# Converting and turning the next graph's adjacency earlier in a four-layer graph kernel

## The chip, the cores and the metric

The kernel runs on one core of a Trainium2 chip. The metric is the device time of one execution in microseconds. The engines are named as the profile names them: PE (TensorE matrix multiplies) with PEld (its weight loads), DVE (VectorE), ACT (ScalarE), POOL (GpSimd), and SP (SyncE), which issues the DMA transfers. The engines run their own instruction lists in order and meet only at semaphores.

## The reference, cut to what matters

There are 16 graphs of 512 nodes with 64 features each. Four graph layers follow one another, each with a residual and a layer norm. The change touches the work of the first two layers.

```python
# layer 0: thin the neighbourhoods, then a weighted sum of three quantiles
# over each node's remaining neighbours, for each feature
neigh = (adj_ > 0) & ~eye
rem = neigh & (sk > 1) & (rank % sk == sk - 1) & mask[:, :, None]
rem = rem | jnp.swapaxes(rem, 1, 2)
vals = jnp.where(nd[..., None], x[:, None, :, :], jnp.inf)
s = jnp.sort(vals, axis=2)
...
h = jax.nn.relu((x + agg) @ W1 + b1);  y = (h @ W2 + b2) * mask
# layer 1: symmetric-normalised graph convolution
row_sum = jnp.sum(adj, axis=-1)                # of adj + identity
out = relu(norm_adj @ (x @ kernel))
x = _layernorm(x + ...)                        # after each layer
```

`adj` comes as float32, one 1 MB matrix for each graph. Layers 2 and 3 read it again, from a bf16 copy that the kernel itself stores.

## The kernel before

**Before the graphs.** All features are sorted once by a sorting network (up to about 300 us), and the ranks of the nodes are found by replaying it backwards. Quantiles of a node are then found by counting which ranks its neighbours hold.

**One stage for each graph.** From about 520 to 2700 us the kernel goes through the 16 graphs, one stage of some 140 us each. Stage b has two parts. `select` runs DVE through four tiles of the graph's counts. `region`, the mixed part, weaves four graphs together: for graph t = b DVE turns the picked words into ranks (`bits_first`, `pop`, `narrow` and so on); for graph p = b + 1 the neighbourhood is prepared; for graph l = b - 1 PE and ACT look up values by one-hot matrices, in 48 *units*; for graph d = b - 2 the dense part of layers 0 and 1 runs (`dense_first`, `dense_second`, `ffn_end`, `dense_turn`, `gcn_start` and on).

**A unit** is, on PE, `spread(u + 2)` (2 matrix multiplies into the single bank `bcast`, L637), `away(u)` (L654) and `lookup(u)` (4 multiplies, L665), with `total` (L677) after each fourth. On ACT it is a pair: `hot` (L1078) of unit u, then `prod` (L1071) of unit u - 2. ACT frees `bcast` for PE's next `spread`, so the two engines go in step. ACT has to be two units ahead in its count, which is why it calls `units(l, STEP[n] + 2)` where PE calls `units(l, STEP[n])`. `STEP` is a table of unit numbers that says where in the row of units each other piece of work stands: STEP[2], STEP[3] and STEP[5] are units 24, 26 and 29.

**The adjacency of the next graph, p,** takes this way. SP loads the float32 matrix into `adj_f` (the trace calls its memory `late`) when DVE has done its last selection of graph t. ACT converts it to `adj_b` in four instructions that also sum the rows (`convert`, L974). PE turns it by 16 transposes, four tiles of four (`turn_adj`, L562), into the two banks of `ring`. ACT copies each tile to `neigh_t` (`keep_turned`, L986). SP then stores `neigh_t` to DRAM (`store_adj`, L429) for the later layers. DVE removes the diagonal from `neigh_t` in place, and so has to wait until the store has read it:

```python
def clear_own(b):
    dve.wait_ge(S["adjT_ev"], NT * b + NT)
    dve.wait_ge(S["adj_out"], 16 * b + 16)      # the store has landed
    for j in range(NT):
        own_block = neigh_t[:, j, P * j:P * j + P]
        did(tt(own_block, own_block, identb[:, :], ALU.is_gt))   # L1424
```

Behind it DVE finishes the first norm of graph d (`gcn_start`, L1672), for which PE waits in `dense_turn` (L702); PE waits for `clear_own` itself in `count_neighbours` (L584). From there PE counts (`count_up`, L594), ACT makes `apart_of` (L1001), DVE marks dropped neighbours in two pairs of instructions (`drop`, L1445), PE and ACT put both directions together, and DVE takes the limits of the quantiles (`limits`, L1456).

**On ACT** `root_of(d, 0)` (L1086), a square root that waits for DVE's semaphore `z_ready` (set behind L1666, the end of `ffn_end`), stands behind the second `keep_turned`.

Of the kernel before, what the change touches and what calls it, by code (L numbers as in the profile page):

```python
# [40 lines left out]
STEP = [LATE + n for n in (0, 1, 2, 4, 6, 7, 9, 11, 13, 14, 15, 17, 19, 21)]  # L41
# [80 lines left out]
def by_vector(l):  # L122

    return l == B - 1
# [15 lines left out]
def build(nc, x_in, adj_in, mask_in, w0a, b0a, w0b, b0b, k1, gamma, beta, w2, b2,  # L140
          w3a, b3a, w3b, b3b, w_ih, b_ih, w_hh, b_hh, out):
    ctx = ExitStack()
    with ctx:
# [379 lines left out]
        def _(pe):  # L523
# [43 lines left out]
            def units(l, n):  # L567

                while l is not None and issued[0] < n:
                    u = issued[0]  # L570
                    if u + 2 < UNITS:
                        spread(l, u + 2)
                    away(l, u)
                    lookup(l, u)
                    if u % 4 == 1 and u >= 5:
                        total(l, u // 4 - 1)
                    issued[0] += 1
# [50 lines left out]
            def spread(l, u):  # L628

                k, g8 = unit(u)  # L630
                at = P * (g8 % 4)
                to, behind = spread_bank(l, u)
                if u >= behind:
                    pe.wait_ge(S["hot_ready"], UNITS * l + u - behind + 1)
                for h in range(2):
                    r = 32 * (2 * h + g8 // 4)
                    ins = mm(to[:, h, :], sel_a[r:r + 32, at:at + P], idx_t[r:r + 32, k, :], start=True, stop=True, tile_position=(r, 0))  # L637
                ins.then_inc(S["bc_ps"], 1)
# [147 lines left out]
            def region(t, p, l, d):  # L786
# [4 lines left out]
                units(l, STEP[1])  # L791
                if d is not None:
                    dense_second(d)
                units(l, STEP[3])
                if p is not None:
                    turn_adj(p, 0, 2)
                units(l, STEP[3] + 1)
                if p is not None:
                    turn_adj(p, 2, NT)
                units(l, STEP[5])  # L800
# [65 lines left out]
            for b in range(B):  # L866
                l, d = b - 1 if b else None, b - 2 if b > 1 else None
                select(b, l)
                region(b, b + 1 if b + 1 < B else None, l, d)
# [78 lines left out]
        def _(act):  # L948
# [23 lines left out]
            def convert_one(b, i):  # L972

                run(adj_b[:, i, :], adj_f[:, i, :], ACT.Copy, accum_out=rowsum[:, b, i:i + 1]).then_inc(S["adjb_ready"], 1)  # L974

            def convert(b):

                act.wait_ge(S["adj_loaded"], 16 * b + 16)
                act.wait_ge(S["rs_ps"], NT * b)
                for i in range(NT):  # L980
                    convert_one(b, i)
# [6 lines left out]
            def keep_turned(b, lo, hi):  # L988

                if lo == 0:  # L990
                    act.wait_ge(S["cw_ps"], NT * CW * b)
                for j in range(lo, hi):
                    keep_one(b, j)
# [62 lines left out]
            def units(l, n):  # L1056

                while l is not None and spread_to[0] < min(n, UNITS + 2):
                    u = spread_to[0]
                    if u < UNITS:  # L1060
                        spread(l, u)
                    if u >= 2 and not by_vector(l):
                        evict(l, u - 2)
                    spread_to[0] += 1
# [66 lines left out]
            def region(t, p, l, d):  # L1131

                units(l, STEP[0] + 2)
                if d is not None:
                    hidden(d)
                units(l, STEP[3] + 2)
                if p is not None:
                    convert(p)
                    keep_turned(p, 0, 2)
                units(l, STEP[3] + 3)  # L1140
                if p is not None:
                    keep_turned(p, 2, NT)
                if d is not None:
                    root_of(d, 0)
                units(l, STEP[5] + 2)
# [56 lines left out]
            for b in range(B):  # L1202
                l, d = b - 1 if b else None, b - 2 if b > 1 else None
# [737 lines left out]
```

## Time and profile before

| | |
|---|---|
| median of 3 runs | 3187.29 us (3184.47 to 3189.19) |
| the profiled execution | 3195.59 us, span 3193.8 us |
| busy, share of the span | PE 70%, DVE 88%, ACT 62%, POOL 0% |
| chain that ended last, by engine | PE 44%, DVE 32%, ACT 13%, issue 7% |
| granted TensorE clock, mean | 0.816 of full speed |

The share of busy time is a mean over parts with different limits: the sort (DVE), the graph stages, and a last part (from about 2890 us) that PE sets. In a timeline a row gives the start, the busy time and, in square brackets, how long the engine sat idle before it and who released it. Stages are named below by the moment at which their store (L429) is issued.

### The profile page before, as it was taken

What the parts mean: (1) busy time and instruction counts of PE and PEld (TensorE: products, weight loads), DVE (VectorE), ACT (ScalarE), POOL (GpSimd) and SP (SyncE); (2) the same over time, 40 slices, a digit from 0 to 9 for tenths busy, and PEclk for the clock granted to TensorE, in tenths of its full rate; (3) what the DMA queues carried; (4) which work ended last, traced back from release to release, by engine and by line L of the source; (5) the groups of instructions that cost most, each with busy time, mean ns of one, the idle gap of its engine ahead of it and who ended that gap; (6) DMA issues with size and microseconds to landing.
All of it is one profiled execution on the core that took longest, in us unless ns stands there. A gap on an engine that the chain in (4) does not pass through costs nothing.

```text
span 3193.8 us, 45583 instructions
## 1 busy us (share of the span) xinstructions
PE 2251.2 (70%) x16081; PEld 1000.7 (31%) x16234; DVE 2805.5 (88%) x5398; ACT 1991.7 (62%) x3077; POOL 12.4 (0%) x24
## 2 busy tenths in 40 slices
PE   0000014387888988888888988888898889776996
PEld 0000002232333333333333333333333333224674
DVE  7999998998999989899999999999898999545776
ACT  2111443278787887778788877878788877741322
POOL 0000000000000000000000000000000000000000
PEclk6555557688998989899999989899898989886777
DMA  3001000000101001010100101010100100000101
GB/s 68 0 0 26 31 0 0 22 24 11 37 8 34 13 29 33 10 33 12 36 11 31 21 21 33 12 37 9 32 15 27 34 10 19 10 20 27 40 26 40
DMA packets 126915, 72.05 MB, mean 23 GB/s; under 512 B 95512, under 2 KB 110058, under 8 KB 126698
## 3 DMA queue, kind: packets, MB, share of 16 engines
q1 hardware_dynamic: 122570, 68.23, 8.3%
q8 instruction: 121, 1.98, 0.3%
q10 hardware_dynamic: 4128, 1.05, 0.2%
q14 instruction: 96, 0.79, 0.1%
HBM read 41.05 MB, written 15.58 MB: 18 GB/s over the span
## 4 chain that ended last, share of the span: by engine, by line
PE 44%; DVE 32%; ACT 13%; issue 7%; SPq 2%; DMA 1%; DVEq 0%; ACTq 0%
PE ring L624 10%; PE rows L665 8%; ACT hot L1078 6%; PE bcast L637 5%; PE found_bank L677 5%; DVE keys L1326 3%; DVE keys L1327 3%; PE bcast L748 2%; PE bcast L757 2%; PE bank L919 2%; ACT prod L1071 2%; DVE picked L1524 2%; DVE delta L1367 2%; DVE delta L1365 1%; DVE perm L1369 1%
## 5 line engine op out<-in xcount | busy, mean ns | idle before, releaser
L1078 ACT ACTIVATE hot<-bcast,consts 128x1024 f16<-128x1024 f32 x744 | 830.7, 1117 | 136.0 <-PE bcast L637 135.5
L665 PE MATMUL rows<-hot,table 128*64 128x512 f16 x3072 | 525.7, 423 | 0.0
L624 PE MATMUL ring<-member,neigh_t 128*128 128x512 bf16 x1925 | 488.9, 392 | 40.0 <-issue 15.1
L1071 ACT ACTIVATE prod<-rows 128x512 f32<-128x512 f32 x720 | 431.1, 599 | 10.4 <-PE rows L665 10.4
L637 PE MATMUL bcast<-idx_t,consts 32*128 32x512 f16 x1488 | 311.3, 415 | 159.6 <-ACT hot L1078 158.0
L654 PE MATMUL rows<-fine_rows,consts 32*128 32x512 bf16 x768 | 316.3, 412 | 18.8 <-DMA fine_rows<-turned 18.1
L562 PE MATMUL ring<-identb,adj_b 128*128 128x128 bf16 x256 | 33.1, 258 | 368.9 <-ACT adj_b L974 357.6
L624 PEld LDWEIGHTS ring<-member,neigh_t 128*128 128x128 bf16 x2048 | 187.4, 101 | 318.8 <-issue 100.2
L677 PE MATMUL found_bank<-prod,consts 128*32 128x512 f32 x1536 | 240.2, 702 | 11.3 <-ACT prod L1071 10.5
L637 PEld LDWEIGHTS bcast<-idx_t,consts 32*128 32x128 f16 x1488 | 70.8, 92 | 499.0 <-ACT hot L1078 332.2
L1524 DVE TENSOR_TENSOR picked<-picked 128x3072 uint16<-128x3072 uint16 (+2 forms) x192 | 209.5, 1091 | 11.2
L1046 ACT ACTIVATE words<-ring 128x512 uint16<-128x512 f32 x256 | 153.4, 600 | 97.9 <-PE ring L624 79.4
L665 PEld LDWEIGHTS rows<-hot,table 128*64 128x64 f16 x3072 | 115.1, 112 | 190.6 <-issue 186.6
L968 ACT ACTIVATE keys<-keys 128x1024 f32<-128x1024 f32 (+7 forms) x72 | 35.5, 544 | 216.2 <-DVE keys L1327 216.2
L562 PEld LDWEIGHTS ring<-identb,adj_b 128*128 128x128 bf16 x256 | 19.6, 111 | 406.1 <-issue 332.7
L1014 ACT ACTIVATE swap<-swapped 128x2048 f16<-128x2048 uint8 (+8 forms) x45 | 73.8, 1643 | 111.5 <-DVE delta L1367 105.1
L1046 ACT ACTIVATE late<-ring 128x512 bf16<-128x512 f32 x128 | 76.9, 601 | 75.4 <-PE ring L624 73.3
L1516 DVE TENSOR_TENSOR picked<-below,words 128x2880 f16<-128x2880 bf16 x64 | 106.1, 1658 | 7.2
L1415 DVE TENSOR_TENSOR member<-words,shares 128x3072 bf16<-128x3072 bf16 x64 | 112.0, 1751 | 0.0
L1490 DVE TENSOR_TENSOR picked<-below,late 128x3072 uint16<-128x3072 bf16 x64 | 112.0, 1751 | 0.0
L1518 DVE TENSOR_TENSOR picked<-below,late 128x3072 uint16<-128x3072 bf16 x64 | 112.0, 1750 | 0.0
L1508 DVE TENSOR_TENSOR picked<-picked,first_at 128x2880 bf16<-128x2880 bf16 x64 | 106.1, 1658 | 2.2
(347 smaller groups left out, 4326.8 us busy)
## 6 DMA issues: line engine op xcount, KB each, us to landing
late<-in_adj_dram SPq DMA_DIRECT2D x16, 1024.0 KB, 5.4
adjt_d<-neigh_t SPq DMA_DIRECT2D x16, 512.0 KB, 2.7
fine_rows<-turned SPq DMA_DIRECT2D x512, 8.0 KB
fine_rows<-turned SPq DMA_DIRECT2D x512, 16.0 KB
turned<-adjt_d SPq DMA_DIRECT2D x16, 512.0 KB, 3.5
adj_s<-adjt_d SPq DMA_DIRECT2D x16, 512.0 KB, 3.8
xt_d<-keys SPq DMA_DIRECT2D x2, 1024.0 KB, 10.5
parts_d<-parts SPq DMA_DIRECT2D x4, 512.0 KB, 6.9
```

What stands on the lines that cost most here:

```text
L624: ins = mm(ring[u % 2][:, :], kept_t[:, j, P * i:P * i + P], member[:, j, n // 2, 512 * (n % 2):512 * (n % 2) + 512], start=(j == 0), stop ...
L637: ins = mm(to[:, h, :], sel_a[r:r + 32, at:at + P], idx_t[r:r + 32, k, :], start=True, stop=True, tile_position=(r, 0))
L654: mm(rows[u % 2][:, :], sel_f[r:r + 32, :], fine_rows[r:r + 32, 2 * k + ROW_SLOT[g8], :], start=True, stop=False, tile_position=(r, 0), sk ...
L665: ins = mm(rows[u % 2][C * h:C * h + C, :], table[:, s, GROUPS * h + g8, :], hot[:, u % HOT, h, :], start=False, stop=(s == 1), skip_group ...
L677: mm(found_bank[to:to + 32, :], sum_to[:, g8 % 4, :], prod[:, u % DEEP, :], start=(m == 0), stop=(u >= UNITS - 4), skip_group_check=True). ...
L1046: run(dst, ring[u % 2][:, :], ACT.Copy).then_inc(S["cw_ev"], 1)
L1071: run(prod[:, u % DEEP, :], rows[u % 2][:, :], ACT.Relu).then_inc(S["prod_by_act"], 1)
L1078: run(hot[:, u % HOT].rearrange(flat), spread_bank(l, u)[0][:, 0:2, :].rearrange(flat), ACT.Relu, bias=eq_bias[:, :]).then_inc(S["hot_read ...
L1415: tt(member[:, j, 1:4, :].rearrange("p s (g c) -> p s g c", g=G), own[:, :, :].unsqueeze(1).to_broadcast([P, 3, G, C]), shares[:, :, j, :] ...
L1490: did(tt(picked[:, w], below[:, :], change[:, w, :].unsqueeze(1).to_broadcast([P, TAUS, G * C]), ALU.mult))
L1518: tt(picked[:, 2], below[:, :, :], change[:, 2, :].unsqueeze(1).to_broadcast([P, TAUS, G * C]), ALU.mult).then_inc(S["mask_used"], 1)
L1524: then(tt(a[:, :, 0:n], a[:, :, 0:n], a[:, :, n:2 * n], ALU.bitwise_xor))
```

## The change

`convert` and `turn_adj`/`keep_turned` stand elsewhere in the row of units of each mixed part. Nothing is added, removed or resized. On ACT `convert` moves up by three units (from behind unit count 28 to behind 25), the two `keep_turned` by two (28 to 26, 29 to 27). On PE the two halves of `turn_adj` move up by two units each (26 to 24, 27 to 25). `root_of(d, 0)` stays behind unit count 29. DVE's and SP's programs are the same; SP's store follows the last copy by its semaphore. In the first mixed part there are no units, so nothing moves there, and the last two have no next graph.

```diff
@@ TensorE, region
-                units(l, STEP[3])
+                units(l, STEP[2])
                 if p is not None:
                     turn_adj(p, 0, 2)
-                units(l, STEP[3] + 1)
+                units(l, STEP[2] + 1)
                 if p is not None:
                     turn_adj(p, 2, NT)
                 units(l, STEP[5])
@@ ScalarE, region
                     hidden(d)
-                units(l, STEP[3] + 2)
+                units(l, STEP[2] + 1)
                 if p is not None:
                     convert(p)
+                units(l, STEP[2] + 2)
+                if p is not None:
                     keep_turned(p, 0, 2)
+                units(l, STEP[2] + 3)
+                if p is not None:
+                    keep_turned(p, 2, NT)
                 units(l, STEP[3] + 3)
-                if p is not None:
-                    keep_turned(p, 2, NT)
                 if d is not None:
                     root_of(d, 0)
```

On ACT, in the mixed part, from the pair behind `hidden` and its first pair up to `root_of`, there stood before (L1078 and L1071 are a pair of a unit, L974 `convert`, L986 the copies, L1086 the root):

```order
L1078 ACTIVATE hot<-bcast,consts 128x1024
L1071 ACTIVATE prod<-rows 128x512
L1078 ACTIVATE hot<-bcast,consts 128x1024
L1071 ACTIVATE prod<-rows 128x512
L1078 ACTIVATE hot<-bcast,consts 128x1024
L1071 ACTIVATE prod<-rows 128x512
L974 ACTIVATE adj_b,rowsum<-late 128x512 x4
L986 ACTIVATE neigh_t<-ring 128x512 x2
L1078 ACTIVATE hot<-bcast,consts 128x1024
L1071 ACTIVATE prod<-rows 128x512
L986 ACTIVATE neigh_t<-ring 128x512 x2
L1086 ACTIVATE inv<-small 128x4
```

And from the same place there stands now:

```order
L974 ACTIVATE adj_b,rowsum<-late 128x512 x4
L1078 ACTIVATE hot<-bcast,consts 128x1024
L1071 ACTIVATE prod<-rows 128x512
L986 ACTIVATE neigh_t<-ring 128x512 x2
L1078 ACTIVATE hot<-bcast,consts 128x1024
L1071 ACTIVATE prod<-rows 128x512
L986 ACTIVATE neigh_t<-ring 128x512 x2
L1078 ACTIVATE hot<-bcast,consts 128x1024
L1071 ACTIVATE prod<-rows 128x512
L1078 ACTIVATE hot<-bcast,consts 128x1024
L1071 ACTIVATE prod<-rows 128x512
L1086 ACTIVATE inv<-small 128x4
```

The four conversions come three pairs earlier, the copies two, and two pairs now stand between the last copy and the root.

On PE, behind unit 23 of the same part, there stood before (L637, L654, L665 are one unit, L677 a `total`, L562 eight of the transposes):

```order
L637 MATMUL bcast<-idx_t,consts 128x512 x2
L654 MATMUL rows<-fine_rows,consts 128x512
L665 MATMUL rows<-hot,table 64x512 x4
L637 MATMUL bcast<-idx_t,consts 128x512 x2
L654 MATMUL rows<-fine_rows,consts 128x512
L665 MATMUL rows<-hot,table 64x512 x4
L677 MATMUL found_bank<-prod,consts 32x512 x4
L562 MATMUL ring<-identb,adj_b 128x128 x8
L637 MATMUL bcast<-idx_t,consts 128x512 x2
L654 MATMUL rows<-fine_rows,consts 128x512
L665 MATMUL rows<-hot,table 64x512 x4
L562 MATMUL ring<-identb,adj_b 128x128 x8
```

And now:

```order
L562 MATMUL ring<-identb,adj_b 128x128 x8
L637 MATMUL bcast<-idx_t,consts 128x512 x2
L654 MATMUL rows<-fine_rows,consts 128x512
L665 MATMUL rows<-hot,table 64x512 x4
L562 MATMUL ring<-identb,adj_b 128x128 x8
L637 MATMUL bcast<-idx_t,consts 128x512 x2
L654 MATMUL rows<-fine_rows,consts 128x512
L665 MATMUL rows<-hot,table 64x512 x4
L677 MATMUL found_bank<-prod,consts 32x512 x4
```

Each half of the transposes comes two units and a `total` earlier.

## Rows read from the trace of the kernel before

**Rows 1.** Busy time of each engine, stretch 703 to 2700 us, core 0.

```profile
core 0: us, PE busy (x) PEld busy (x) DVE busy (x) ACT busy (x) POOL busy (x), PEclk, DMA share, GB/s
703.00:2700.00 1997.00, 1724.56 (x12421) 699.24 (x12558) 1841.02 (x3689) 1595.72 (x2503) 0.00 (x0) 0.91 0.09 23
```

**Rows 2.** Waits of DVE, 703 to 2700 us: total us, times, longest us.

```profile
DVE adj_b L1445 <- ACT apart_of L1001: 19.8, 14, 3.5
DVE neigh_t L1424 <- DMA adjt_d<-neigh_t: 15.9, 11, 4.2
DVE mult L1456 <- PE ring L615: 12.2, 14, 1.3
```

**Rows 3.** Timeline of DVE: start us, busy us, work, [idle before <-releaser].

```profile
1440.63 0.17 DVE L1666 TENSOR_SCALAR small<-moments 128x4 f32<-128x4 f32 x1
...
1445.44 0.63 DVE L1424 TENSOR_TENSOR neigh_t<-neigh_t,identb 128x128 bf16<-128x128 bf16 x4 [0.91 <-DMA adjt_d<-neigh_t]
...
1462.65 1.41 DVE L1445 SCALAR_TENSOR_TENSOR adj_b<-apart_of,small,adj_b 128x512 bf16<-128x512 f16 x2 [0.74 <-ACT apart_of L1001]
...
1475.33 0.30 DVE L1456 TENSOR_SCALAR mult<-ring 128x4 uint16<-128x4 f32 x3 [0.83 <-PE ring L615]
```

**Rows 4.** Timeline of SP's queue in the same stage.

```profile
1417.79 0.40 SPq L393 DMA_DIRECT2D late<-in_adj_dram  x1
1442.65 0.35 SPq L429 DMA_DIRECT2D adjt_d<-neigh_t  x1
```

**Rows 5.** The page's DMA issues: times, KB each, median us to landing.

```profile
late<-in_adj_dram SPq DMA_DIRECT2D x16, 1024.0 KB, 5.4
adjt_d<-neigh_t SPq DMA_DIRECT2D x16, 512.0 KB, 2.7
```

**Rows 6.** Timeline of ACT in the same stage.

```profile
1430.93 1.11 ACT L1078 ACTIVATE hot<-bcast,consts 128x1024 f16<-128x1024 f32 x1 [1.89 <-PE bcast L637]
...
1436.07 0.62 ACT L974 ACTIVATE adj_b<-late 128x512 bf16<-128x512 f32 x1
...
1438.43 0.19 ACT L974 ACTIVATION_READ_ACCUMULATOR adj_b<-late 128x1 f32 x1
1439.00 1.08 ACT L986 ACTIVATE neigh_t<-ring 128x512 bf16<-128x512 bf16 x2 [0.38 <-PE ring L562]
...
1441.44 1.11 ACT L986 ACTIVATE neigh_t<-ring 128x512 bf16<-128x512 bf16 x2
1442.39 0.24 ACT L1086 ACTIVATE inv<-small 128x4 f32<-128x4 f32 x1
```

**Rows 7.** Timeline of PE in the same stage.

```profile
1430.78 1.07 PE L665 MATMUL rows<-hot,table 128*64 128x512 f16 x4
...
1439.94 0.62 PE L562 MATMUL ring<-identb,adj_b 128*128 128x128 bf16 x8
...
1444.12 1.07 PE L665 MATMUL rows<-hot,table 128*64 128x512 f16 x4
1446.18 0.59 PE L584 MATMUL ring<-consts,neigh_t 128*128 128x1 bf16 x16 [1.00 <-DVEq L1277]
1447.58 1.03 PE L702 MATMUL bcast<-ident,pre 128*64 128x128 f32 x4 [0.80 <-DVEq L1277]
```

**Rows 8.** Timeline of DVE in three other stages.

```profile
1158.76 0.63 DVE L1424 TENSOR_TENSOR neigh_t<-neigh_t,identb 128x128 bf16<-128x128 bf16 x4 [0.94 <-DMA adjt_d<-neigh_t]
...
1177.49 1.41 DVE L1445 SCALAR_TENSOR_TENSOR adj_b<-apart_of,small,adj_b 128x512 bf16<-128x512 f16 x2 [1.59 <-ACT apart_of L1001]
...
1304.03 0.63 DVE L1424 TENSOR_TENSOR neigh_t<-neigh_t,identb 128x128 bf16<-128x128 bf16 x4 [4.19 <-DMA adjt_d<-neigh_t]
...
1585.39 0.63 DVE L1424 TENSOR_TENSOR neigh_t<-neigh_t,identb 128x128 bf16<-128x128 bf16 x4
```

**Rows 9.** Timeline of PE, stage 1301.24.

```profile
1304.77 0.59 PE L584 MATMUL ring<-consts,neigh_t 128*128 128x1 bf16 x16 [1.53 <-DVEq L1277]
1306.16 1.03 PE L702 MATMUL bcast<-ident,pre 128*64 128x128 f32 x4 [0.80 <-DVEq L1277]
```

**Rows 10.** Busy time and granted clock between `clear_own` and the second `drop`, two stages.

```profile
1158.76:1177.49 18.73, 16.20 (x161) 7.07 (x162) 14.98 (x41) 12.62 (x19) 0.00 (x0) 0.77 0.01 1
1445.44:1462.65 17.21, 14.85 (x161) 6.95 (x162) 14.98 (x41) 12.50 (x19) 0.00 (x0) 0.85 0.01 1
```

More of the change, by code:

```diff
@@ L1135, in region @@
                     hidden(d)
-                units(l, STEP[3] + 2)
+                units(l, STEP[2] + 1)
                 if p is not None:
                     convert(p)
+                units(l, STEP[2] + 2)
+                if p is not None:
                     keep_turned(p, 0, 2)
-                units(l, STEP[3] + 3)
+                units(l, STEP[2] + 3)
                 if p is not None:
                     keep_turned(p, 2, NT)
+                units(l, STEP[3] + 3)
                 if d is not None:
```

## The prediction

> **What bounds the kernel now.** I read the busy times of the graph stages first. From 703 to 2700 us DVE is busy for 1841.0 of 1997 us, 92%, PE for 1724.6 and ACT for 1595.7 [rows 1]. So DVE sets the pace of these stages, and what can be won is what makes DVE stand still. The view of its waits names three groups that recur in all or most stages: 19.8 us ahead of the second `drop`, 15.9 us ahead of `clear_own` for the landing of the adjacency store, and 12.2 us ahead of `limits` [rows 2]. The change aims at the second. Next I read the timelines around one store, in the stage of 1442.65, to see what makes the store late and who follows it.
>
> DVE comes to `clear_own` at 1445.44 - 0.91 = 1444.53 and waits 0.91 us [rows 3]. The store was issued at 1442.65 [rows 4] and takes 2.7 us to land [rows 5], so it is free at about 1445.4. It was issued right behind ACT's last copy, which ends at 1441.44 + 1.11 = 1442.55 [rows 6]. Behind `clear_own` PE is waiting twice: 1.00 us for L584 and 0.80 us for L702 [rows 7]. So PE is there before DVE, and a later DVE makes a later PE. From L702 the path runs over PE's and ACT's units and counts to the second `drop` at 1462.65, where DVE waits 0.74 us, and to `limits` at 1475.33, where it waits 0.83 us [rows 3]. Behind that DVE goes without a long wait to the next `clear_own`: from the second `drop` at 1462.65 [rows 3] to 1585.39 [rows 8] are 122.74 us, and in that next stage the store had landed and it didn't wait. I worked the same distance out for the other stages, less the wait at its end: it is 122.3 to 123.0 in eleven of the twelve, which is what DVE's own work takes. A stage is therefore: DVE's fixed part, the wait for the store, and the stretch from `clear_own` to the second `drop`. The last runs from 17.21 us (1445.44 to 1462.65) [rows 3] to 18.73 us (1158.76 to 1177.49) [rows 8], with a mean of 17.9 over 13 stages.
>
> **How much earlier is the store?** The same instructions run, so nothing is removed or added in busy time. On ACT the four conversions take 1436.07 to 1438.62, 2.55 us, and PE has its transposes waiting for them, after which ACT idles 0.38 us [rows 6]. In the new place they stand ahead of the pair that starts at 1430.93. ACT sits idle there for 1.89 us, from 1429.04 [rows 6], since PE is busy with `dense_second`. The adjacency is in memory by then: issued at 1417.79 [rows 4], 5.4 us to land [rows 5], 1423.2, so 5.8 us to spare. The conversions run from 1429.04 to 1431.6, and the pair behind them starts 0.7 us late. Without that cover they would cost the full 2.55. PE ends unit 23 at 1430.78 + 1.07 = 1431.85 [rows 7] and finds `adj_b` ready. Eight transposes take 0.62 us at full clock [rows 7], at half clock at most double, 1.2: done at 1433.0. ACT has its pair until 1433.2, two copies to 1434.3 (1.08 us [rows 6]), a pair to 1435.9 (a pair takes 1.1 + 0.5), and two copies, 1.11 us [rows 6], to 1437.0. PE's second half waits for the first copies and runs 1434.3 to 1435.5, in time. Against 1442.55 the last copy is 5.5 us earlier, and the store lands at 1437.1 + 2.7 = 1439.8, 4.7 us ahead of DVE. SP has nothing else to issue between, so the earlier store passes no other transfer.
>
> **What that gives.** All 14 stages that have units and a next graph are touched; 11 waited. The longest wait is 4.19 us, in the stages of 1301.24 [rows 8] and 2291.11. A store 5.5 us earlier covers 4.19 as well, with 1.3 to spare. So the first term is -15.9 us [rows 2], and it has to be looked at whether the path behind can follow. In ordinary stages L584 moves from 1446.18 to 1445.27; PE was free at 1445.18 [rows 7], and gets free earlier now, because the conversions no longer stand in ACT's row of pairs there. In the two long stages DVE would be ready for L584 at 1304.77 - 4.19 = 1300.58, and PE was free only at 1303.24 [rows 9]. PE's row of units gets shorter by what ACT's gap takes up: between 1.0 (PE at half clock, its own work binding) and 2.5 (all of the conversions). L584 then ends at 1303.24 - 1.0 + 0.59 = 1302.83 at worst, L702 follows against 1306.16 [rows 9]: a gain of 3.3, at best the whole 4.19. I take 0.8 us off for each of the two, for PE is at half clock there and so nearer to the worst: +1.6 us. The stretch behind L702 starts from the same state as before, as PE and ACT have both run their units up to that point and stand waiting; I put its change at 0 with a bound on either side from the clock (next paragraph). The root of `root_of(d, 0)` now comes to a semaphore that DVE hasn't set, and ACT will wait there; priced below as a rival, at 0 in the sum. In sum: -15.9 + 1.6 = -14.3 us, from the profiled execution's 3195.6 to 3181.3. It lay 8.3 us above the median of the runs; the same difference taken from 3187.3 is **3173 us**, 0.45% faster.
>
> **The clock, from both sides.** What differs between 17.21 and 18.73 us is TensorE's granted clock: 0.85 in the first stretch, 0.77 in the second, with the same 161 multiplies and DVE's same 14.98 us [rows 10]. The levels in it are 1.2 and 2.4 GHz, and the low one comes behind idle time of PE. The change makes PE arrive earlier at L584 than DVE, so that its idle time, until now partly spread among the units, gathers ahead of L584. If every one of 13 stages went as the worst seen, the stretches would cost (18.73 - 17.93) x 13 = +10.4 us; if every one went as the best, -9.4 us.
> The Trainium skill, page "TensorE: Matmul & The Clock Gate", part 1 on the clock gate, says that "the default state is throttled, and activity releases the throttle"; it speaks against the change, since the gap ahead of the path's first multiplies gets longer. By that rule the first bound holds and the sum is -14.3 + 10.4 = -3.9 us, 3183 us. The trace agrees that a low clock costs 1.5 us here [rows 10], but it shows no stage with the longer gap.
>
> **Rivals.**
> *The forecast's case*, store wait gone, clock as mixed as before: 3173, own range 3166 to 3180. 0.73.
> *The clock eats it.* As above, 3183 us, within 0.2%; in the best direction instead 3164. For it: the longer gap. Against: even now the stages differ among themselves with PE idle 1.0 to 1.8 us ahead of L702 [rows 7, 9], and total idle gets less. Bad direction 0.15; good direction, to 3164, 0.04.
> *The wait only moves to the second `drop`.* If the path to it did not start at L702 but at PE's units, `drop` would wait 15.9 us more and nothing is won: 3187. Against: the 0.80 us for which PE waits for DVE at L702 [rows 7, 9]. 0.04.
> *Slower: ACT blocked at the root.* The root was reached at 1442.39, behind `z_ready` at 1440.80 [rows 3, 6]. Now ACT comes there about 1437.0 + 2 x 1.6 = 1440.2 and in late stages has to wait for DVE, and behind it stand the next two pairs, PE's `spread` and the last lookup ahead of L584. From the root's end at 1442.63 [rows 6] to the lookup's end at 1445.19 [rows 7] are 2.56 us; with 0.24 for the root and up to 0.4 for the semaphore that is 3.2 us behind `z_ready`. DVE needs 1445.27 - 1440.80 = 4.47 us from there to L584. So 1.3 us are to spare. It decides from 4.5 us on, and would make the kernel slower by more than 0.2% only when it took 4.47 + 1.1 (the gain of a stage) + 0.5 = 6.1 us in every stage, double what the rows give: 3194 or more. 0.04.
>
> **How the numbers follow.** This kernel's measurement can tell about 0.2%, 6.4 us, from no change. Faster by more is under 3180.9: the forecast's case and the good clock, 0.77. Same: clock and moved wait, 0.18. Slower: 0.05, the blocked root with the tail of the clock. The range reaches to both clock bounds with a little of the run spread: 3162 to 3185.
>
> **What the changed profile would show.** Right: the row of L1424 waiting for the store gone; the issue of L429 some 5 us earlier against the adjacency's load (19 to 20 us behind L393 instead of 24.9); L974 directly behind a gap of ACT that is gone or small; a new wait of ACT at L1086 for DVE, under 3 us; PE's wait ahead of L584 longer in ordinary stages; DVE's waits at L1445 and L1456 near 19.8 and 12.2 us; a stage without slow spots 140.0 us. Wrong: L1445's wait grown by as much as L1424's fell, with a granted clock under 0.80 between them; or L584 with no idle time ahead of it in most stages, which would mean that PE and ACT, and not DVE, set the start of the path.

## The result and the profile after

Over 20 runs of each the changed kernel takes 3183.45 us (3177.74 to 3187.85), the kernel before 3189.70 us (3184.47 to 3198.96). The ratio is 0.9979 with an interval of 0.9972 to 0.9986: 0.21% faster, 6.3 us. The profiled execution took 3183.33 us against 3195.59, 12.3 us less. Why the two differences are not the same is a main finding below. Two executions in the experiments fell far out and are in no ratio: 4484.57 us, one of nine of `fill_before` (its median of 3190.61 counts it; without it, it is 3190.09), and 3498.51 us, one of 23 of the kernel before in the third set.

In the file of the changed kernel the lines of DVE's program stand three higher (L1427 is `clear_own`, L1448 `drop`, L1459 `limits`, L1504 and L1507 take up words and late of a tile). The page's busy times of the changed kernel:

```profile
PE 2234.6 (70%) x16081; PEld 1004.7 (32%) x16234; DVE 2805.6 (88%) x5398; ACT 1987.2 (62%) x3077; POOL 12.4 (0%) x24
```

Its waits of DVE from 700 to 2700 us (total us, times, longest us):

```profile
DVE adj_b L1448 <- ACT apart_of L1001: 18.3, 14, 2.6
DVE mult L1459 <- PE ring L615: 11.0, 13, 0.9
DVE late L1507 <- ACT late L1046: 9.4, 9, 1.4
...
DVE late L1504 <- ACT words L1046: 5.1, 6, 1.0
```

Against [rows 2] the wait for the store is gone, all 15.9 us of it, and the other two are a little less. What grew is the pair at L1504 and L1507, 14.5 us here. The kernel before has less at the same two places (L1501 and L1504 there):

```profile
DVE late L1504 <- ACT late L1046: 3.4, 5, 1.5
DVE late L1501 <- ACT words L1046: 0.9, 1, 0.9
```

Over all the graph stages, from 600 us on, it is 14.9 us against 4.3; below, the waits "for words and late" are always this sum. DVE has them when the second tile's *chunks* come late: the counts of the next graph, which PE makes (L624) and ACT copies into `words` and `late` (L1046).

The stage whose store is issued at 1288.27, changed kernel, in the timelines of SP, ACT, PE and DVE, one after the other:

```profile
1269.56 0.40 SPq L393 DMA_DIRECT2D late<-in_adj_dram  x1
1288.27 0.35 SPq L429 DMA_DIRECT2D adjt_d<-neigh_t  x1
```

```profile
1280.69 0.64 ACT L974 ACTIVATE adj_b<-late 128x512 bf16<-128x512 f32 x1
...
1292.76 0.20 ACT L1086 ACTIVATE inv<-small 128x4 f32<-128x4 f32 x1 [1.11 <-DVEq L1280]
```

```profile
1297.11 0.59 PE L584 MATMUL ring<-consts,neigh_t 128*128 128x1 bf16 x16 [2.14 <-DVEq L1280]
1298.50 1.03 PE L702 MATMUL bcast<-ident,pre 128*64 128x128 f32 x4 [0.80 <-DVEq L1280]
```

```profile
1296.37 0.63 DVE L1427 TENSOR_TENSOR neigh_t<-neigh_t,identb 128x128 bf16<-128x128 bf16 x4
...
1313.96 1.42 DVE L1448 SCALAR_TENSOR_TENSOR adj_b<-apart_of,small,adj_b 128x512 bf16<-128x512 f16 x2 [1.11 <-ACT apart_of L1001]
```

The store comes 18.7 us behind the load, not 24.9 [rows 4], and 8.1 us ahead of `clear_own`, which has no idle time ahead of it. ACT has the new wait at the root, 1.11 us. PE waits 2.14 us ahead of L584 where it waited 1.00, and still 0.80 ahead of L702 [rows 7]: the path starts at DVE, as said. From `clear_own` to the second `drop` are 17.59 us. All of that is as forecast. What is not is half a stage further on, behind the turning of the ranks. Changed kernel, same stage, timelines of PE and then DVE:

```profile
1350.43 0.89 PE L735 MATMUL rows<-identb,idx_home 128*128 128x128 bf16 x8 [1.22 <-ACT turned L1194]
...
1354.47 0.60 PE L733 MATMUL rows<-identh,idx_home 128*128 128x128 f16 x4 [1.09 <-ACT idx_t L1191]
...
1356.80 3.19 PE L624 MATMUL ring<-member,neigh_t 128*128 128x512 bf16 x7 [0.22 <-issue]
```

```profile
1367.23 1.16 DVE L1504 TENSOR_TENSOR late<-words 128x1920 uint16<-128x1920 uint16 x1 [0.98 <-ACT words L1046]
...
1369.94 0.43 DVE L1507 TENSOR_SCALAR late<-late 128x1024 uint16<-128x1024 uint16 x1 [1.45 <-ACT late L1046]
```

And the stage ahead of it, PE, then DVE, and the windows view of the low clock in both stages (busy times, then the granted clock as the third number from the end):

```profile
1215.28 2.56 PE L624 MATMUL ring<-member,neigh_t 128*128 128x512 bf16 x7 [0.22 <-issue]
```

```profile
1226.34 1.16 DVE L1504 TENSOR_TENSOR late<-words 128x1920 uint16<-128x1920 uint16 x1
1227.52 0.43 DVE L1507 TENSOR_SCALAR late<-late 128x1024 uint16<-128x1024 uint16 x1
```

```profile
1353.17:1359.97 6.80, 5.49 (x27) 2.69 (x26) 6.59 (x6) 4.96 (x8) 0.00 (x0) 0.53 0.06 13
1213.07:1219.87 6.80, 6.58 (x43) 3.65 (x43) 6.65 (x6) 4.57 (x8) 0.00 (x0) 0.71 0.05 12
```

While PE turns the ranks it waits for ACT's copies in gaps of 0.4 to 1.2 us, and behind them the clock is low for some microseconds. In the first stage shown this lies on the chunks that follow: the seven multiplies of L624 take 3.19 us, not 2.56, and DVE is there before the words: 0.98 + 1.45 = 2.43 us. In the other stage the low clock starts and ends some 3 us earlier (at 54.0 and 60.8 us behind `clear_own`, not 57.2 and 64.0), and DVE doesn't wait. So it isn't whether the clock falls there, which it does in every stage of this trace, but where in the stage it falls. Of the changed kernel's 14 stages with units six have such waits of 1.7 us or more together, of the kernel before's one.

### The profile page after: what moved, and what is told of

The parts are those of the page before. It is cut to its first block, busy times and chain, and to the rows that moved or that the text cites. A ratio compares the mean times of both kernels' runs of the same rounds, so it can differ in the third digit from the quotient of the medians.

```text
span 3181.5 us, 45583 instructions
## 1 busy us (share of the span) xinstructions
PE 2234.6 (70%) x16081; PEld 1004.7 (32%) x16234; DVE 2805.6 (88%) x5398; ACT 1987.2 (62%) x3077; POOL 12.4 (0%) x24
## 4 chain that ended last, share of the span: by engine, by line
DVE 57%; PE 27%; ACT 8%; issue 6%; SPq 1%; DMA 1%; DVEq 0%; ACTq 0%
PE ring L624 5%; DVE picked L1527 5%; PE rows L665 4%; ACT hot L1078 3%; PE found_bank L677 3%; PE bcast L637 3%; DVE picked L1519 3%; DVE picked L1511 3%; DVE picked L1521 3%; DVE picked L1493 3%; DVE keys L1329 3%; DVE keys L1330 3%; PE bank L919 2%; DVE picked L1499 2%; DVE delta L1370 2%
## 5 line engine op out<-in xcount | busy, mean ns | idle before, releaser
L1078 ACT ACTIVATE hot<-bcast,consts 128x1024 f16<-128x1024 f32 x744 | 831.5, 1118 | 112.8 <-PE bcast L637 112.8
L624 PE MATMUL ring<-member,neigh_t 128*128 128x512 bf16 x1925 | 495.4, 396 | 40.8 <-issue 16.0
L665 PE MATMUL rows<-hot,table 128*64 128x512 f16 x3072 | 515.8, 416 | 0.0
L1071 ACT ACTIVATE prod<-rows 128x512 f32<-128x512 f32 x720 | 432.1, 600 | 10.1 <-PE rows L665 10.1
L637 PE MATMUL bcast<-idx_t,consts 32*128 32x512 f16 x1488 | 309.5, 413 | 169.4 <-ACT hot L1078 167.6
L654 PE MATMUL rows<-fine_rows,consts 32*128 32x512 bf16 x768 | 314.2, 409 | 18.1 <-DMA fine_rows<-turned 18.0
L624 PEld LDWEIGHTS ring<-member,neigh_t 128*128 128x128 bf16 x2048 | 189.3, 102 | 325.0 <-issue 110.0
L562 PE MATMUL ring<-identb,adj_b 128*128 128x128 bf16 x256 | 33.2, 294 | 358.7 <-ACT adj_b L974 347.3
L677 PE MATMUL found_bank<-prod,consts 128*32 128x512 f32 x1536 | 233.1, 683 | 11.2 <-ACT prod L1071 10.4
L637 PEld LDWEIGHTS bcast<-idx_t,consts 32*128 32x128 f16 x1488 | 70.6, 92 | 510.7 <-ACT hot L1078 338.0
L1046 ACT ACTIVATE words<-ring 128x512 uint16<-128x512 f32 x256 | 153.4, 600 | 102.9 <-PE ring L624 84.5
L665 PEld LDWEIGHTS rows<-hot,table 128*64 128x64 f16 x3072 | 114.3, 111 | 188.9 <-issue 184.9
L562 PEld LDWEIGHTS ring<-identb,adj_b 128*128 128x128 bf16 x256 | 22.5, 130 | 381.9 <-issue 332.4
L1046 ACT ACTIVATE late<-ring 128x512 bf16<-128x512 f32 x128 | 76.9, 601 | 75.8 <-PE ring L624 73.7
## 6 DMA issues: line engine op xcount, KB each, us to landing
xt_d<-keys SPq DMA_DIRECT2D x2, 1024.0 KB, 10.4
```

What stands on the lines that cost most here:

```text
L624: ins = mm(ring[u % 2][:, :], kept_t[:, j, P * i:P * i + P], member[:, j, n // 2, 512 * (n % 2):512 * (n % 2) + 512], start=(j == 0), stop ...
L654: mm(rows[u % 2][:, :], sel_f[r:r + 32, :], fine_rows[r:r + 32, 2 * k + ROW_SLOT[g8], :], start=True, stop=False, tile_position=(r, 0), sk ...
L665: ins = mm(rows[u % 2][C * h:C * h + C, :], table[:, s, GROUPS * h + g8, :], hot[:, u % HOT, h, :], start=False, stop=(s == 1), skip_group ...
L677: mm(found_bank[to:to + 32, :], sum_to[:, g8 % 4, :], prod[:, u % DEEP, :], start=(m == 0), stop=(u >= UNITS - 4), skip_group_check=True). ...
L1046: run(dst, ring[u % 2][:, :], ACT.Copy).then_inc(S["cw_ev"], 1)
L1071: run(prod[:, u % DEEP, :], rows[u % 2][:, :], ACT.Relu).then_inc(S["prod_by_act"], 1)
```

## The experiments

All were run beside the kernel before on the same chip. Its median there was 3198.2 us in the first set (`again_before`, `again_after`, `store_early`, `fill_turn`), 3201.6 in the second (`control_after`, `fill_before`, `one_later`, `fill_both`), 3203.2 in the third (`root_later`, `fill_584`, `fill_wide`, `again_before2`); in the fourth (the other profiles) it ran once, 3213.3. The changed kernel's medians are 3183.45, 3184.14 and 3184.47 us (the last with the root moved) on three occasions, so where it was not timed in a set, medians are compared with these; the ratios carry the spread of the kernel before.

**Second profiles of both kernels, unchanged.**

> The kernel before, unchanged, for a second profile. Theory A (the 15.9 us of store waits are typical, and what was lost of them was lost behind the path): the waits ahead of clear_own sum to 14 to 18 us again, and DVE's waits ahead of the second tile's words and late (L1501, L1504) to under 6 us. Theory B (the first profile, 6 us above the median of 20 runs, was an execution with unusually long store waits): the sum is under 11 us. In B the term of the forecast was too large before anything else happened.

> The changed kernel, unchanged, for a second profile. Theory A: no wait ahead of clear_own, and again 4 to 7 of the 14 stages in which DVE waits 2.4 us for the second tile's words and late, with a low granted clock some 57 to 64 us behind clear_own; sum of these waits 10 to 17 us. Rival C (that was chance of one execution): sum under 5 us and a time near 3173 us.

The kernel before took 3196.26 us, with 20.0 us of store waits and 4.2 us at words and late. The changed kernel took 3187.28 us, with none and 13.6 us. So both effects are there again, and theory B falls as it was written; the last group of profiles gives a part of it back.

**The wait away, nothing moved.** The kernel before, with

```diff
 def store_adj(b):
-    hold(sp, S["adjT_ev"], NT * b + NT, S["sp_passed"])
-    sp.dma_start(adjt_d[b], neigh_t[:, :, :]).then_inc(S["adj_out"], 16)
+    hold(sp, S["adjb_ready"], NT * b + NT, S["sp_passed"])
+    sp.dma_start(adjt_d[b], adj_b[:, :, :]).then_inc(S["adj_out"], 16)
...
 def clear_own(b):
     dve.wait_ge(S["adjT_ev"], NT * b + NT)
-    dve.wait_ge(S["adj_out"], 16 * b + 16)
...
 def drop(b, i):
     dve.wait_ge(S["apart_ready"], NT * b + i + 1)
+    if i == 0:
+        dve.wait_ge(S["adj_out"], 16 * b + 16)
```

> The kernel before with its order of units, but the store takes its 512 KB from adj_b, right behind the conversions (the adjacency is symmetric, so the bytes are the same as those of the turned copy), and DVE waits for the store ahead of drop and not ahead of clear_own. So the wait is away and nothing on PE and ACT has moved. clear_own still needs the last copy, some 2.8 us before the old landing. Theory A (all that the change gives is the wait that it takes away): ratio to before 0.9975 to 0.9985, as the changed kernel; where the last copy itself is late (the two long stages) 1.4 us each stay. Rival D (moving the units costs or gives something by itself, ACT's new wait at the root above all): this kernel differs from the changed one's 0.9979 by more than 0.1%: nearer 0.9955 if the moved units cost time, 0.999 or more if they were what helped.

Median 3179.99 us, ratio 0.9941 (0.9918 to 0.9964). DVE's waits, this kernel:

```profile
DVE adj_b L1446 <- ACT apart_of L1001: 18.7, 14, 3.9
DVE mult L1457 <- PE ring L615: 12.5, 14, 1.4
DVE late L1505 <- ACT late L1046: 8.1, 9, 1.4
...
DVE late L1502 <- ACT words L1046: 3.7, 4, 1.0
```

No store wait, and the same waits for words and late, 11.8 us. The range of ratios that I had written down came from the first occasion's 0.9979, and taken by the letter the measured 0.9941 would be rival D's; but against the changed kernel's own ratio of 0.9942 in the next set the two are the same. So within what these ratios can tell, 0.2% or 7 us, what the change gives is the wait that it takes away, and the late chunks are there with nothing on PE and ACT moved. The median is 3.5 to 4.5 us below the changed kernel's; whether the moved units cost that little was not tested.

**The changed kernel timed again, as a control.**

> The changed kernel once more, timed, so that it and the kernels sent with it share one chip: ratio to before 0.995 to 0.999. Theory A: its profile shows no wait ahead of clear_own and 10 to 17 us of waits for the second tile's words and late again.

Median 3184.14 us, ratio 0.9942 (0.9927 to 0.9958), waits at words and late 14.0 us. The changed kernel's time is that of the first occasion within 1 us; the ratio is not, since the kernel before is 12 us slower here.

**Two added multiplies in each gap of the turning.** In the changed kernel, ahead of each of PE's waits for ACT:

```diff
 pe.wait_ge(S["idx_ready"], b + 1)
+if b >= 2:
+    pe.wait_ge(S["gcn_ev"], b - 1)
 for u, k in enumerate(TURN_ORDER):
     if u >= 2:
+        for _ in range(2):
+            mm(dense_bank[:, :], identb[:, :], upper[:, :], start=True, stop=True)
         pe.wait_ge(S["idxT_ev"], TURNS * b + u - 1)
```

> The changed kernel with 14 added multiplies of 128x512 in each graph's turning of the ranks (two ahead of each of PE's waits for ACT there), into a part of the bank bcast that nobody reads; nothing else. They cost PE 0.22 us each at full clock, in gaps of 0.4 to 1.2 us. Theory A (the gain was given back by the low granted clock that these gaps bring, through the first chunks of the next graph): DVE's waits for words and late fall from 14.5 to under 4 us, the clock 53 to 64 us behind clear_own stays at full, and the time falls by 8 to 14 us against the changed kernel, ratio to before 0.994 to 0.9955. Rival E (the waits come from PE's amount of work, not its clock): the added work makes them longer, and the ratio is 0.998 to 1.003.

The edit has one thing more than is said there: PE first waits for `gcn_ev`, so that the multiplies don't write over a part of the bank that is still to be read. In this trace PE never stands at that wait.

Median 3175.64 us, ratio 0.9931 (0.9905 to 0.9957); DVE's waits for words and late 3.1 us where the changed kernel has 13.6 to 14.9. PE behind the turning, this kernel, and the windows view of the same place in the stage as above:

```profile
1350.35 0.60 PE L733 MATMUL bcast<-consts,identb 128*128 128x512 bf16 x2
...
1351.67 1.89 PE L624 MATMUL ring<-member,neigh_t 128*128 128x512 bf16 x8
```

```profile
1348.91:1355.71 6.80, 6.14 (x51) 3.48 (x51) 6.55 (x7) 5.54 (x10) 0.00 (x0) 1.00 0.06 15
```

Eight multiplies of the first chunk now take 1.89 us, where seven took 3.19. From 53 to 64 us behind `clear_own` the granted clock is 1.00 in all 13 of the later stages, where the changed kernel has 0.69 in all of them. More work on PE made the chunks earlier, so it was the clock and not the work (rival E falls). The time is 8.5 us under the changed kernel's 3184.14 of the next set, and the two ranges hardly touch; the ratio is below the range expected, for the same reason as above. Not all of the gain is late chunks: the mean clock behind `clear_own` rose too (0.92 against 0.82 up to the second `drop`), and that stretch became 0.26 us shorter.

**The same added multiplies in the kernel before.**

> The kernel before with the same 14 added multiplies in each turning of the ranks, and nothing moved. Theory A (two separate losses: the late store, and the low granted clock behind the turning of the ranks): the store waits stay, 10 to 20 us, since nothing makes the store earlier, the chunk waits are under 4 us, and the ratio is 0.997 to 1.001, so that the change is worth 0.3 to 0.5% when the other loss is away (against the 0.9931 of the filled changed kernel). Rival F (filling alone does it, the change adds nothing): ratio as that of the filled changed kernel, 0.993 to 0.994.

Median 3190.61 us, ratio 0.9965 (0.9952 to 0.9978). The store waits stay:

```profile
DVE adj_b L1449 <- ACT apart_of L1005: 20.6, 14, 3.7
DVE neigh_t L1428 <- DMA adjt_d<-neigh_t: 20.4, 8, 4.6
```

Both kernels gain from the filling, and the changed one stays 15 us ahead of this one (3175.6 against 3190.6, in two sets). The ratio is a little below the 0.997 expected. Rival F falls. Where this kernel gained I can't say: its waits for words and late are 2.2 us, and the kernel before had only some 4 of them.

**One unit later in place of earlier.** In the kernel before, `STEP[3]` and `STEP[3] + 1` of `turn_adj` become `STEP[3] + 1` and `STEP[3] + 2`, and ACT's two places move by one as well.

> The kernel before with conversions, transposes and copies one unit later in place of earlier. A unit is 1.6 us on ACT. Theory A (DVE's wait for the store is on the path and goes one to one into the time): the store is issued 26.4 us behind the load in ordinary stages where it was 24.9, the waits ahead of clear_own grow by about 1.6 us in each of 14 stages to 36 to 44 us, and the time by 14 to 26 us, ratio 1.004 to 1.009. Rival G (the wait is largely slack that moves between places): the waits grow, the time stays within 0.2%.

Median 3233.89 us, ratio 1.0096 (1.0077 to 1.0116): 32 us slower, more than the 14 to 26 expected.

```profile
DVE neigh_t L1424 <- DMA adjt_d<-neigh_t: 55.2, 14, 7.6
...
DVE late L1504 <- ACT late L1046: 7.4, 6, 1.5
DVE late L1501 <- ACT words L1046: 7.1, 5, 3.3
```

The wait is now in all 14 stages, 55.2 us where profiles of the kernel before have 7.3 to 29.3; the store is issued 27.2 to 28.1 us behind the load in most stages, 3 us later and not 1.6. A stage mean went from 141.6 to 144.9 us. So the wait is on the path, and a unit costs more than ACT's 1.6 us there. And this kernel, whose store wait grew, has as many late chunks as the changed one, 14.7 us. The late chunks are therefore not the price of taking a wait away: they depend on the moment at which each stage meets the low clock, and any change to the length of the stages can bring them or end them. Against the first profile of the kernel before, from 608 us to the last `clear_own`, the store waits are 39.2 us more and the late chunks 10.4, the stretches to the second `drop` 3.6 less. Which part of the additional 1.4 us is the low clock (it is low from 8 us ahead of `clear_own` to 6 behind it in this kernel) I did not separate.

**The root one pair later.** `units(l, STEP[3] + 4)` ahead of `root_of(d, 0)` in the changed kernel.

> The changed kernel with root_of(d, 0) one pair of ACT later, behind unit count 30. In the profiles of the changed kernel ACT waits there for DVE up to 2.6 us a stage. Theory A (that wait lies beside PE's wait for DVE ahead of L584 and costs nothing): the wait at this root falls to near 0.3 us or none, the start of L702 stays 2.13 us behind clear_own, and the time stays within 0.2% of the changed kernel in the same chip's terms (ratio to before 0.994 to 0.999). Rival D (the wait at the root costs part of the gain): 0.3% or more faster than the changed kernel, ratio under 0.992 where the chip's before is near 3200 us.

Median 3184.47 us, ratio 0.9947 (0.9928 to 0.9967), the same as the changed kernel. The waits at this root (0.7 to 2.3 us in most stages before) are gone in all but two stages, and ACT waits as much longer at the next root: 51.4 us in 15 waits for both, against 51.8 us in 25. L702 starts 2.13 us behind `clear_own` as before, in all stages but the first (3.68). The wait at the root costs nothing that these runs can tell.

**Multiplies ahead of the neighbour count.** With those of the turning (`fill_both`), and alone (`fill_584`), in the changed kernel:

```diff
 def count_neighbours(b):
+    if b >= 2:
+        pe.wait_ge(S["adjT_ev"], NT * b + NT)
+        for _ in range(6):
+            mm(ring[0][:, :], identb[:, :], upper[:, :], start=True, stop=True)
     pe.wait_ge(S["neighT_ready"], b + 1)
```

> The changed kernel with the 14 added multiplies in each turning of the ranks, and 6 more of 128x512 ahead of the neighbour count (L584) in each stage, where PE is idle for 1.5 to 2.1 us waiting for DVE. Theory A (the stretch from clear_own to the second drop, 17.1 to 18.7 us, is set by the granted clock, and the idle time ahead of L584 brings the low one): the low clock from about -1 to +6 us around clear_own goes or gets shorter, the stretch falls to a mean of 16.6 to 17.1, and the time by 4 to 10 us against the kernel filled only in the turning. Rival H (the stretch is set by ACT's pairs, the clock hardly matters, and the six multiplies at half clock, 2.6 us, delay L584): the time stays or grows by up to 10 us.

> The changed kernel with only the 6 added multiplies ahead of L584, none in the turning of the ranks. Theory A (two separate effects of the clock, one on each stretch): the stretch from clear_own to the second drop has a mean under 17.3 us where the changed kernel has 17.7, while the waits for the second tile's words and late stay over 6 us; time between the changed kernel and the one with both fillings, 3170 to 3180 us. Rival H (the stretch got shorter only through what the filling in the turning did): stretch 17.6 or more, time as the changed kernel's.

`fill_both`: median 3167.60 us, ratio 0.9903 (0.9880 to 0.9925). `fill_584`: 3165.52 us, ratio 0.9891 (0.9867 to 0.9915). The stretch from `clear_own` to the second `drop` has a mean of 16.83 and 17.07 us against 17.7, and the waits for words and late are 0.7 and 7.4 us. DVE's waits in `fill_584`:

```profile
DVE mult L1463 <- PE ring L619: 13.0, 13, 1.5
DVE adj_b L1452 <- ACT apart_of L1005: 6.7, 9, 1.2
...
DVE late L1511 <- ACT late L1050: 5.1, 5, 1.4
```

Ahead of the second `drop` DVE waits 6.7 us, not 18.3. The mean granted clock of the stretch is 0.95 in `fill_both` and 0.91 in `fill_584`, against 0.82. So here too the clock set the time, and rival H falls. That `fill_584` alone is as fast as both was not expected (3170 to 3180 us were), and their ranges (3162.8 to 3169.9, 3163.4 to 3175.2) don't tell them apart. Both beat the changed kernel by 0.5 to 0.6%.

**More of it.** `fill_both`, and two more in each of units 19 to 23 and 37 to 41, ahead of the multiply of `away`:

```diff
+if 19 <= u < 24 or 37 <= u < 42:
+    for _ in range(2):
+        mm(rows[u % 2][:, :], identb[:, :], upper[:, :], start=True, stop=True)
 mm(rows[u % 2][:, :], sel_f[r:r + 32, :], ...
```

> The kernel with both fillings, and 2 more added multiplies of 128x512 in each of units 19 to 23 and 37 to 41, where ACT's pairs set the pace and PE is idle for 0.65 us of 1.6. 20 multiplies a stage, 4.3 us at full clock. Theory A (what is left of low clock behind DVE's selection and behind limits comes from this idle time, but no longer lies on the path in most stages): the mean granted clock rises above 0.85, and the time falls by only 0 to 5 us against both fillings, 3163 to 3168 us. Rival I (PE is so near its bound there that the added work delays the chunks or the dense part): 3170 us or more.

Median 3193.98 us (3187.23 to 3203.06), ratio 0.9979 (0.9959 to 0.9999), 26 us slower than `fill_both`, in the next set: rival I. The mean clock did rise, to 0.856 from 0.839, but

```profile
DVE mult L1470 <- PE ring L619: 31.4, 14, 2.3
```

the wait for `limits` is 31.4 us, not 12.8, and DVE's part of a stage is 123.7 us, not 122.4. PE's count for `limits` stands behind the filled units, and a higher clock does not pay for the work. That is part of the loss. Between the two profiled executions (38.9 us of span) 17.6 us lie ahead of the last `clear_own`, and the other 21.3 behind it, which I did not take apart.

**How much does the kernel before vary?** Four more profiles of it, and one of the changed kernel.

> The kernel before, a third profile. If it is near 3196 us again: 14 to 20 us of store waits, with two or more stages of 145 us and a wait over 3.8 us. If it falls to 3190 us or less: fewer of these long stages, under 12 us of store waits; that would say that the spread between executions of the kernel before is the number of its long stages.

> The kernel before, a fourth profile. If the store waits make its executions differ: time = 3174 + (sum of waits ahead of clear_own, 7 to 22 us) within 4 us, so 3181 us goes with about 7 and 3196 us with 16 to 20. If something else does, the sum does not follow the time.

> The kernel before, a fifth profile; the same relation, within 4 us.

> The kernel before, a sixth profile; the same relation, within 4 us.

> The changed kernel, a fourth profile: no wait ahead of clear_own, 10 to 17 us of waits for the second tile's words and late, 3178 to 3188 us.

| profiled execution | us | store waits | words and late | mean stretch to second drop |
|---|---|---|---|---|
| before, again 2 | 3180.76 | 7.3 | 8.9 | 17.63 |
| before, first | 3195.59 | 16.0 | 4.3 | 17.93 |
| before, again | 3196.26 | 20.0 | 4.2 | 17.82 |
| before, again 4 | 3196.51 | 19.7 | 4.2 | 18.01 |
| before, again 5 | 3208.83 | 23.7 | 4.6 | 18.08 |
| before, again 3 | 3213.77 | 29.3 | 4.2 | 18.24 |
| changed, four executions | 3183.33 to 3187.63 | 0 | 13.6 to 14.9 | 17.70 to 17.73 |

The fastest and the slowest of them, DVE's waits for the store:

```profile
DVE neigh_t L1424 <- DMA adjt_d<-neigh_t: 7.3, 8, 2.3
...
DVE neigh_t L1424 <- DMA adjt_d<-neigh_t: 29.3, 13, 4.2
```

The time follows the sum of the store waits, but steeper than one to one. My relation of 3174 us plus the waits was made from the first three profiles; of the three that could test it, it holds within 4 us for one (again 4) and is 10 to 11 us short for the two slowest (again 3 and 5). So it failed as stated. There the stretch to the second `drop` is longer as well; 0.6 us in 13 stages is 8 us. And what lies behind the last `clear_own` differs too, 612.4 us in the fastest and 621.5 in again 5.

The fastest of these executions of the kernel before, 3180.76 us, is faster than any of the changed kernel's four, with 7.3 us of store waits still in it. It has fewer late chunks (8.9 us) and a short end. So the change does not win in every execution; it wins in the median. In the slowest execution stages of 141.4 and 145.3 us alternate, five of the latter, each with a store wait of 3.8 to 4.2 us; the fastest has none. What sets a long stage apart can be seen in the first profile: ahead of the wait of 4.19 us (stage 1301.24) the clock is low from 17.2 to 3.5 us before `clear_own`, and the store comes 28.2 us behind the load; in the next stage, with 0.91 us, it is low from 15.2 to 8.4 us before, and the store comes after 24.9. So one and the same program ends between 3181 and 3214 us, and its long stages go with where the low clock falls; no run forced that pattern, so the cause is argued here and not shown. The store wait is the place at which the executions of the kernel before differ most. The changed kernel's four profiled executions lie within 5 us, its 20 timed ones within 10.

## Why the prediction had the mechanism of the wait right and the gain too large

**Right.** That DVE bounds the stages; that the store is issued some 5.5 us earlier (24.9 to 18.7 us behind the load, 6.2); that 4.19 us of wait would be covered too; that all 15.9 us go; that the conversions fit into ACT's gap; that ACT waits anew at the root, under 3 us, and without a cost that the runs can tell (`root_later`); that L702 and with it the path start at DVE; that the way along PE and ACT to the second `drop` would keep its length: 17.71 us mean, after 17.93. `one_later` and `store_early` show the wait on the path from both sides.

**Wrong in size, first: DVE's own part of a stage was taken as fixed.** The prediction said of the distance from the second `drop` to the next `clear_own` that it "is what DVE's own work takes" and put no term there. It is that only as long as the chunks are there in time. The sign of it lay in the prediction's own count: eleven of the twelve stages had 122.3 to 123.0 us, and the twelfth, 125.0, was passed over. It is the stage in which the kernel before had these very waits, 0.89 + 1.45 = 2.34 us:

```profile
1935.41 1.16 DVE L1501 TENSOR_TENSOR late<-words 128x1920 uint16<-128x1920 uint16 x1 [0.89 <-ACT words L1046]
...
1938.12 0.43 DVE L1504 TENSOR_SCALAR late<-late 128x1024 uint16<-128x1024 uint16 x1 [1.45 <-ACT late L1046]
```

In the changed kernel the waits for words and late are 14.9 us, against 4.3. Between the `clear_own` at some 608 us and the last one, the two first profiles differ by 11.9 us: -15.6 in idle time ahead of `clear_own`, -3.4 in the stretches, +7.1 in DVE's part, of which the late chunks are +8.5 (2.2 more come behind the last `clear_own`) and everything else about -1.5. The clock rival had the size of the loss, 10.4 us and 3183 us, by luck, for it had it at the wrong place: it looked only at the stretch behind L584, where the clock cost nothing more, and not at the one behind the turning of the ranks. `fill_turn` shows the cause of the late chunks, and with `fill_584` and `fill_both` that the clock was to be had at both places.

**A small term that was not there.** The prediction took 0.8 us off for each of two long stages, +1.6 us, since PE might not follow. In the changed kernel PE stands waiting for DVE ahead of L584 in every stage (1.47 to 2.14 us), and L702 starts 2.13 us behind `clear_own` in all 13: the term is 0.

**Wrong in size, second: the profiled difference was carried over to the median.** "The same difference taken from 3187.3" assumed that the profiled execution, 8.3 us above the median, was above it for reasons that the change leaves alone. It was above it in part by the very waits that the change removes. The table shows it: 7.3 us of them at 3180.8, 16 to 20 at 3196; an estimate from these two for the median of 20 runs, 3189.7, is 12 to 14 us. In part only, for of the 14.8 us between the fastest profile and the first, the store waits are 8.5 us; the stretches are 4.7 more, the late chunks 4.8 less, and 4.2 lie behind the last `clear_own`. The forecast for the profiled execution, 3181.3, was 2.0 us off, in part by luck, as the late chunks took 10.6 us that were in no term and the shorter stretches and DVE's other work gave back some 5; for the median, 3173.0, it was 10.5 us off. The size of the gain is thus a matter of the occasion: 0.21% on the first, which the forecast was for, 0.58% (0.9942) on a chip on which the kernel before took 3201.6 us. The forecast of 0.45% is more than twice the first and lies between the two, and the range, 3162 to 3185, held the time.

On what the prediction took from the Trainium skill, page "TensorE: Matmul & The Clock Gate", part 1, that activity releases the throttle: `fill_turn` agrees, the granted clock from 53 to 64 us behind `clear_own` being 1.00 where the changed kernel has 0.69. What I let the rule say of this change did not come, that the longer gap ahead of L584 would lengthen the path behind it: the mean stretch went from 17.93 to 17.71 us.

What stays open: why the kernel before is slower on some occasions than on others (medians from 3189.7 to 3203.2 us), that is, what picks the pattern of stages at the start; what `fill_before` gained by; and why a unit later costs 3 us of store time in `one_later`.

## What to carry to other kernels

That the bound engine shows no waits in a stretch does not make the stretch its own work alone: look how close the data that it takes up comes, and look at the one stage that doesn't fit. Any change ahead of it moves everything else against the low-clock stretches. Where executions differ by more than the change is worth, take several profiles before sizing a term, and ask whether the term is what makes them differ. Six added multiplies in one of PE's waiting gaps gave more on top (0.6%) than the reordering itself had given on the first occasion (0.2%). In the two places where they gained, work of PE that is on the path follows the gap; in units that were near PE's bound they cost 26 us.

## What was not expected of the hardware

The granted clock was low behind gaps of only 0.4 to 1.2 us in the turning. In the stage shown it fell at 1353.6, and PE had been busy for 1.91 of the 4 us ahead of that. A program without any change in its data or instructions took 3181 to 3214 us, 1%, and its long stages were those that met the low clock at another moment; patterns of two (141.4 and 145.3 us) or three stages (140.1, 142.4 and 140.7 us in the changed kernel) repeat to 0.1 us. A higher mean clock (0.856) went with a slower kernel.
